# Second attention: place of the head 2 and 3 copies in steps without a product, and VectorE taking both parts of the last weight chunks

## The reference

```python
def _L1_attn_ref(hidden_states, qkv_w, qkv_b, out_w, out_b):
    ...
    qkv = hidden_states @ qkv_w + qkv_b
    q, k, v = jnp.split(qkv, 3, axis=-1)          # each (b, 256, 32 heads, 16)
    ...
    q = _rope(q, cos, sin)
    k = _rope(k, cos, sin)
    scores = jnp.einsum('bqhd,bkhd->bhqk', q, k) * scale
    scores = scores + (1.0 - causal) * MASK_VAL
    probs = jax.nn.softmax(scores, axis=-1)
    ctx = jnp.einsum('bhqk,bkhd->bqhd', probs, v).reshape(b, s, e)
    return ctx @ out_w + out_b

def _L1_ffn_ref(x, U1, V1, U2, V2, b1, b2):
    P = jnp.einsum('bsh,hr->bsr', x, U1)
    H = jnp.einsum('bsr,rf->bsf', P, V1) + b1
    gate, up = (H[..., :INTER], H[..., INTER:])
    act = jax.nn.silu(gate) * up
    Z = jnp.einsum('bsi,ir->bsr', act, U2)
    return jnp.einsum('bsr,rh->bsh', Z, V2) + b2
...
x = x + 0.5 * _L0_ffn_ref(_layernorm(x), ...)
x = x + _L0_attn_ref(_layernorm(x), ...)
x = x + 0.5 * _L0_ffn_ref(_layernorm(x), ...)
x = x + 0.5 * _L1_ffn_ref(_layernorm(x), ...)
x = x + _L1_attn_ref(_layernorm(x), L1_attn_qkv_w, L1_attn_qkv_b, L1_attn_out_w, L1_attn_out_b)
x = x + 0.5 * _L1_ffn_ref(_layernorm(x), ...)
```

## Time and profile before

| | us |
|---|---|
| median of 3 runs | 1808.23 (1807.68 to 1809.49) |
| profiled execution | 1806.9 |
| its span on the core | 1805.0 |
| TensorE busy (matmuls) | 1741.9 (97%) |
| VectorE busy | 1098.3 (61%) |
| ScalarE busy | 1083.7 (60%) |
| GpSimd busy | 930.7 (52%) |

### The profile page before, as it was taken

How to read it: one execution, slowest core, us unless ns; L and a number is a source line. 1 busy time by engine, 2 the same in 40 slices (tenths; PEclk the granted TensorE clock), 3 DMA queues, 4 the chain that set the end, 5 groups by cost and what they waited for, 6 DMA issues and landing times.

```text
span 1805.0 us, 32175 instructions
## 1 busy us (share of the span) xinstructions
PE 1741.9 (97%) x11116; PEld 1519.4 (84%) x11116; DVE 1098.3 (61%) x3305; ACT 1083.7 (60%) x3077; POOL 930.7 (52%) x1170
## 2 busy tenths in 40 slices
PE   7989999999999999999999999999999998899798
PEld 6779999999999999899899899989888776677567
DVE  6664565556456545645654664565566677888756
ACT  3355666566556656655765664566563263888964
POOL 5555545455544555554555554455542254877850
PEclk9999999999999999999999999999999999999999
DMA  4300021012001101200110120020011121000101
GB/s 150 108 24 7 14 64 36 1 41 65 7 18 59 36 1 48 65 1 19 59 36 1 48 65 1 19 72 23 1 59 59 42 66 41 1 2 2 37 12 47
DMA packets 35424, 65.79 MB, mean 36 GB/s; under 512 B 4032, under 2 KB 4672, under 8 KB 35264
## 3 DMA queue, kind: packets, MB, share of 16 engines
q1 hardware_dynamic: 35264, 63.73, 11.2%
HBM read 61.62 MB, written 2.10 MB: 35 GB/s over the span
## 4 chain that ended last, share of the span: by engine, by line
PE 74%; ACT 8%; DVE 8%; issue 6%; POOL 3%; DMA 0%; SPq 0%; DVEq 0%; POOLq 0%; ACTq 0%
PE bank L363 57%; PE bank L1102 6%; PE bank L1089 4%; PE bank L1104 3%; ACT s L1216 2%; ACT s L1739 2%; PE bank L1673 1%; DVE h L760 1%; PE bank L1644 1%; PE bank L1660 1%; DVE work L771 1%; DVE work L1321 1%; POOL h L838 1%; ACT h L683 1%; DVE x L1390 1%
## 5 line engine op out<-in xcount | busy, mean ns | idle before, releaser
L363 PE MATMUL bank<-W,oT 128*128 128x512 f32 x1632 | 432.1, 400 | 0.6 <-DVE x L1876 0.6
L1427 POOL TENSOR_TENSOR qk<-work,qk 128x512 fp32r<-128x512 f32 (+1 forms) x160 | 193.1, 1207 | 429.3 <-ACT qk L1207 429.3
L363 PEld LDWEIGHTS bank<-W,oT 128*128 128x128 f32 x1632 | 288.3, 189 | 48.5 <-DVE x L1876 1.1
L1223 ACT COPY pt<-bank 128x384 f32<-128x384 f32 x256 | 122.0, 477 | 322.7 <-PE bank L1089 322.0
L1419 POOL TENSOR_TENSOR work<-work,table 128x512 f32<-128x512 f32 (+1 forms) x160 | 191.3, 1195 | 133.7 <-ACT work L1202 133.7
L1216 ACT ACTIVATE s<-s,neg_max 128x128 f32<-128x128 f32 (+1 forms) x512 | 227.5, 445 | 50.1 <-DVE neg_max L1335 49.0
L363 PE MATMUL bank<-W,xnA 128*128 128x320 f32 (+1 forms) x1056 | 191.7, 336 | 2.8 <-DVE xnA L348 2.2
L1312 DVE TENSOR_TENSOR work<-bank,table 128x512 f32<-128x512 f32 (+1 forms) x160 | 102.0, 637 | 129.4 <-ACT work L1202 129.4
L363 PEld LDWEIGHTS bank<-W,xnA 128*128 128x128 f32 x1056 | 166.7, 189 | 15.9 <-DVE xnA L348 3.4
L363 PE MATMUL bank<-qk 128*128 128x256 f32 (+1 forms) x768 | 166.0, 351 | 0.9 <-POOL qk L1427 0.9
L1355 DVE COPY lvv<-bank 128x320 f32<-128x320 f32 x128 | 62.9, 491 | 169.6 <-PE bank L363 169.1
(11 more groups left out here) (111 smaller groups left out, 3499.6 us busy)
## 6 DMA issues: line engine op xcount, KB each, us to landing
raw<-in_weights SPq DMA_DIRECT2D x215, 256.0 KB, 2.7
x<-in_x SPq DMA_DIRECT2D x8, 256.0 KB, 5.6
out<-x SPq DMA_DIRECT2D x8, 256.0 KB, 2.1
row<-in_bias_rows SPq DMA_DIRECT2D x5, 256.0 KB, 2.9
table<-in_constants SPq DMA_DIRECT2D x4, 240.0 KB, 3.1
b_qk<-in_bias_rows SPq DMA_DIRECT2D x1, 512.0 KB, 3.7
b_val<-in_bias_rows SPq DMA_DIRECT2D x1, 256.0 KB, 2.8
table<-in_constants SPq DMA_DIRECT2D x1, 66.0 KB, 2.5
```

Source lines behind the costliest of these rows:

```text
L363: last = nc.tensor.matmul(out_ap, lhs(i), rhs(j), start=start and k == 0, stop=stop and k == 2)
L1223: nc.scalar.copy(pt0[:, k, :], bank[PT][:, 0:3 * P]).then_inc(a_pt, 1)
L1427: nc.gpsimd.tensor_tensor(lo, work[:, 2 + s, st.columns(what)], hi.bitcast(F32), ALU.subtract).then_inc(a_rope_lo, 1)
```

## The change

In a step without a product the copy of head 3 of quad n-1 stands on VectorE ahead of the last minima and not behind them, and the copy of head 2 stands on ScalarE between the exponentials of heads 0 and 1 and not behind both. In all steps with a weight chunk ScalarE and GpSimd no longer split it: VectorE writes its high part behind its second reciprocal and its low part behind the tile's and `oT`'s low parts, ahead of the rope's last addition and the addition of an output product.

```diff
--- before.py
+++ after.py
@@ -257,6 +257,11 @@
                 turn = 0 if g is None else g
                 act.wait_ge(raw_loaded[s], 16 * (before + 1) + turn * (16 * per))
                 nc.scalar.copy(dst[HI], raw[:, s, :]).then_inc(w_hi, 1)
+
+            def split_hi_vector(self, dve, j, dst):
+                s, before, _, _ = self.at[j]
+                dve.wait_ge(raw_loaded[s], 16 * (before + 1))
+                nc.vector.tensor_copy(dst[HI], raw[:, s, :]).then_inc(w_hi, 1)
 
             def split_lo(self, dve, j, dst, g=None):
                 s = self.at[j][0]
@@ -1748,10 +1753,14 @@
                 b_scalar_norm(act, *tile)
             if heads and at_once:
                 b_scalar_masks(act, *heads)
+            no_product = before and fill_of(n) is None
             if here:
                 exponentials(0)
+            if no_product:
+                b_pt_copy(act, n - 1, 2)
+            if here:
                 exponentials(1)
-            if before:
+            if before and not no_product:
                 b_pt_copy(act, n - 1, 2)
             if heads and not at_once:
                 b_scalar_masks(act, *heads)
@@ -1764,8 +1773,6 @@
                 group = n // 2 - 1
                 act.wait_ge(b_pv, group + 1)
                 nc.scalar.copy(oT1[HI][:, group % ORING, :], bank[OUT1][:, 0:SEQ]).then_inc(b_o_hi, 1)
-            for i in last_splits(n):
-                st_f1b.split_hi(act, i, chunk(W, LAST[i]))
             if n == QUADS - 1:
                 ffn1b.low_rank_hi(act, ffn1b.z0, 0, FILL)
             if here:
@@ -1912,13 +1919,17 @@
                 minima(1)
             if tile and not later:
                 b_vector_norm(dve, *tile)
+            no_product = before and fill_of(n) is None
             if here:
                 minima(2)
+            if no_product:
+                b_pt_copy(dve, n - 1, 3)
+            if here:
                 minima(3)
             if heads and not at_once:
                 b_vector_keys(dve, *heads)
             halves = fill and fill[0] != "first" and before and not norm_of(n - 1)
-            if before and not halves:
+            if before and not halves and not no_product:
                 b_pt_copy(dve, n - 1, 3)
             if here:
                 inverses(0)
@@ -1934,6 +1945,8 @@
                 b_vector_biased(dve, *fill[1:])
             if here:
                 inverses(1)
+            for i in last_splits(n):
+                st_f1b.split_hi_vector(dve, i, chunk(W, LAST[i]))
             if tile and later:
                 b_vector_norm(dve, *tile)
             if before and n % 2 == 0:
@@ -1944,6 +1957,8 @@
                                         ALU.subtract).then_inc(b_o_lo, 1)
             if n == QUADS - 1:
                 ffn1b.vector_first(dve, FILL)
+            for i in last_splits(n):
+                st_f1b.split_lo(dve, i, chunk(W, LAST[i]))
             if roped:
                 b_vector_turned(dve, *roped)
             if fill and fill[0] == "out":
@@ -2018,8 +2033,6 @@
                 normalise(3)
             for i in norms_after(n)[1] if norms_after(n) else ():
                 ln_power(pool, norm_no(norms_after(n)[0], i), i % 2)
-            for i in last_splits(n):
-                st_f1b.split_lo_pool(pool, i, chunk(W, LAST[i]))
```

## The result

The changed kernel takes 1821.39 us (median of 4 runs, 1820.21 to 1822.53) against 1808.86 us for the kernel before beside it (1807.68 to 1809.53). The ratio is 1.0071, with a 95% interval from 1.0059 to 1.0083: slower by 12.5 us. The direction was as forecast, the size wasn't: 1815.1 had been forecast, and 1821.39 lies above the range (1810.5 to 1821.0). The profiled execution took 1820.2 us with a span of 1818.4, against 1806.9 and 1805.0.

What follows compares the result with a forecast made beforehand. TensorE was taken to bound steps with a product, a ScalarE-VectorE loop the others. Splits +7.5 and copies -0.6 gave +6.9 us: 1813.8 on the profiled clock, 1815.1 with 1.3 for the median; range 1810.5 to 1821.0.

Steps and rivals of the forecast that it cites:

- What bounds the steps: Steps with a product go at TensorE's pace, others at a ScalarE-VectorE loop without room behind the second reciprocal.
- the walk: Step-by-step count of the splits' delay over steps 22 to 30, reaching +7.5 us at step 30.
- Step 30: Step with one chunk and an addition: 6.9 us against 6.0 forecast, bringing the accumulated delay to +7.5 us.
- The lengths: VectorE's time per part: high 0.45 us for a first chunk, 0.6 each in pairs; low 0.75 us.
- heavy collision: Rival: low parts and second high parts of pairs wait amid GpSimd's multiplications, +4.9 us, 1820 us; chance 0.19.
- Copies sooner: Steps 5 and 6: earlier head copies start the weighing sooner, -0.6 us together; nothing more in steps 25 to 28.
- small loss: Rival: lower bounds of the splits hold and TensorE's slow stretch in step 25 goes, +3.0 us, 1811.2 us; chance 0.16.
- faster: Rival: ScalarE alone sets the loop, gains in steps 5, 6, 25 to 28 and clock, -3.9 us, 1804.3 us; chance 0.08.

Runs made afterwards that it cites:

- The shifted pair: The changed kernel with one chunk of step 29 split earlier: two chunks each in steps 27 and 28, one in 29; 1818.73 us, ratio 1.0055.
- splits ahead: The changed kernel with both parts of each chunk on VectorE ahead of its second reciprocal; 1817.18 us, ratio 1.0039.
- low parts alone: The changed kernel, copies moved, with only the low parts on VectorE and the high parts back on ScalarE; 1815.94 us, ratio 1.0050.

## Why the forecast was right and wrong

**What bounds the steps: right.** That there was no room behind the second reciprocal, and none between the addition and the product, is what the trace after shows step by step. Six of the nine steps come within 0.55 us of the walk; step 22 (7.55 forecast, 7.58 measured) and steps 27 and 28 (0.2 us under it) best. The product of step 23 starts 1.47 us later by the two timelines, 1.2 once the 0.24 us by which step 22 began later are taken off, and 1.2 was forecast.

**Step 30: the term that failed most.** The walk had 6.9 us and it took 9.31. The reciprocal came 5.34 us behind the first exponential (1728.52 to 1733.86), not 4.01, since the copy of head 2 had to wait for TensorE's turning at 1.2 GHz, and `oT` (1735.62) waited for the weighing behind the slow product. I had named the clock as what could make the forecast wrong upwards and hadn't put it into the range. The shifted pair measures it: 2.4 us. This is the step of the forecast that failed: it priced the wait ahead of the product and put the clock behind it at nothing. With it the forecast would have been 1817.5, still 3.9 us short.

**The lengths: right for a lone high part, too kind for the others.** A first high part takes 0.38 us where it meets nothing, 0.29 to 0.35 from its start to the next one's, against the 0.45 taken. The formula of the Trainium skill ("VectorE: DVE Perf Modes", section "⚠️ The TRN2 errata — SBUF-src ops pay a fixed extra latency per instruction"), 58 + 512/2 cycles of 0.96 GHz, had given an estimate of 0.33 us; the trace's 0.38 lies somewhat above it. But "it starts before GpSimd has its next multiplication" holds only where GpSimd is idle. In steps 23 and 24 GpSimd is adding a bias row (L2030) when VectorE's reciprocal ends, and in step 26 it is still multiplying:

```profile
1678.26 1.45 POOL L2030 TENSOR_TENSOR x<-x,row 128x512 f32<-128x512 f32 x1
...
1679.21 0.78 DVE L264 CAST W<-raw 128x512 fp32r<-128x512 f32 x1
...
1680.03 1.20 DVE L270 TENSOR_TENSOR W<-raw,W 128x512 fp32r<-128x512 f32 x1
...
1685.56 1.27 POOL L2030 TENSOR_TENSOR x<-x,row 128x512 f32<-128x512 f32 x1
...
1685.96 1.16 DVE L264 CAST W<-raw 128x512 fp32r<-128x512 f32 x1
```

Both conversions end 0.28 to 0.29 us behind the end of GpSimd's addition (1679.71 and 1686.83), little less than the 0.38 us that one takes alone, so nearly the whole conversion lies behind the addition. The rule of the Trainium skill ("SBUF — State Buffer", section "🔬 SBUF: two separate sides"), an exclusive lock whose loser is blocked for the other's whole instruction, is borne out by these rows and by the medians of 375 and 848 ns at two places; it should have been in the sum at each place where GpSimd was at work. Read from start to start on the path, the parts take 0.7 us more than the walk gave in step 23, 0.6 in step 24, 0.4 in step 26 and 0.5 in step 29, 2.2 in all, less than half of the heavy collision's 4.9; in steps 25, 27 and 28 they take 0.8 less.

**Two smaller terms.** In step 25 the walk had the second reciprocal 4.01 us behind the first exponential, as in step 27. It came at 4.57, since VectorE's own statistics of a tile stand ahead of it there (and did before: 4.19). In step 29 it came at 5.09 and not 4.74, as the copy of head 2 waited for TensorE, which was at 1.2 GHz behind a wait of 1.79 us in step 28.

**Copies sooner: wrong for steps 5 and 6, and more elsewhere.** Their -0.6 isn't there. Steps 5 and 6 together took 11.67 us before and 11.87 in the kernel with the splits alone; in the nine traces with both copies they took 11.54 to 13.10, 12.2 in the mean. The weighing of step 5 did start 1.0 us sooner (1556.87), 0.86 counted from the step's first exponential, as forecast (0.88), and at full clock. But in five of the nine traces, after among them, the slow clock then came in step 6 (0.57 to 0.75), in two it stayed in step 5 (0.72), and even the two without it gained only 0.1 us. What the copies are seen to bring alone, they bring in step 25 (1.1 us), where in the changed kernel VectorE's splits hide it. The rivals *small loss* and *faster* had this clock among their terms; the other term of *faster*, ScalarE as the sole bound, fell.

**The account**, by the windows: the nine steps took 4.9 us more than the walk. The clock of step 30 is 2.4 of it, the lengths of the splits 2.2 less 0.8, the later reciprocals of steps 25 and 29 0.9, and 0.2 is left over. Steps 0 to 21 gave 0.2 us back and not 0.6, and 1.3 us stand ahead of the first step and behind step 30, of which the forecast had none. Only the clock's term is isolated by a run; the others are read off the steps of one trace, while runs of one kernel scatter by 2 us and more.

## What to carry to other kernels

Before moving work onto an engine, look at which side of that engine's last wait its idle time stands, and look in every step. Here 1.5 to 2.2 us of idle time lay ahead of the second reciprocal in steps 27 to 30 and at most 0.3 us in steps 22, 23 and 25; behind it there was none. So a chunk behind it added 0.6 us in step 27 and 1.2 in step 22, and ahead of it nothing in step 27 and 1.5 in step 23. Check also whether GpSimd is at work at that place: the same conversion took 375 ns at the median where it wasn't and 848 where it was. Add TensorE's slow clock to the price of a new wait, as a possible cost and not a sure one. Of this change the copies alone are worth keeping (ratio 0.9985, 0.9977 to 0.9994); the splits are better left to ScalarE and GpSimd, which had the room.

## What the runs showed of the hardware

- VectorE converts 128x512 f32 SBUF to SBUF in 374 ns with GpSimd waiting and in up to 1159 in after; the subtraction with two SBUF sources takes 632 to 1493 (both in the run with the parts behind the two reciprocals).
- A wait's length alone doesn't tell TensorE's clock: behind 2.89 us it was 0.50 (step 30 of after) and behind 1.42 us 1.00, but it was 0.50 behind 1.79 us too (step 28 of after), and in before it fell behind 2.37 us in step 25 and not behind 2.60 us in step 27.
- Steps 5 and 6 have the same instructions in nine of the kernels here, and their clock still differed, as these windows of step 6 show (after; splits ahead; low parts alone). Single traces differ by up to 1.6 us for it, so a step's gain of that size needs several.

```profile
1560.90:1567.65 6.75, 5.62 (x49) 3.75 (x50) 5.70 (x31) 4.98 (x20) 4.59 (x9) 0.75 0.00 1
```

```profile
1561.62:1569.10 7.48, 6.35 (x47) 4.30 (x48) 6.17 (x33) 5.21 (x21) 5.04 (x9) 0.57 0.00 1
```

```profile
1560.64:1566.56 5.92, 4.28 (x49) 2.74 (x49) 5.12 (x27) 5.20 (x20) 3.75 (x8) 1.00 0.01 1
```
